# Reordering SyncE's loads of A and x in a fused LoRA and residual kernel

## The reference

```
x = x + einsum('bct,bcd->bdt', x, cond_W[cond_id])
x = x + (x @ W.T + b + 2 * (x @ A[slot]) @ B[slot])      # per sample, slot = adapter id
```

## Time and profile before

| what | value |
|---|---|
| median of 3 runs | 84.96 us (84.85 to 85.13) |
| the profiled execution | 84.99 us |
| its span, first to last instruction | 83.2 us |
| PE busy | 79.4 us (95% of the span) |
| DVE busy | 60.2 us (72%) |
| ACT busy | 52.3 us (63%) |
| POOL busy | 33.7 us (41%) |
| granted TensorE clock | 1.000 |

### The profile page before, as it was taken

One profiled execution on the slowest core, in us unless ns is written; L12 is line 12 of the kernel. 1 busy time (PEld: TensorE's weight loads), 2 busy tenths in 40 slices (PEclk: granted clock), 3 DMA queues, 4 the chain that ended last, 5 costly groups with the idle time before them and its releaser, 6 DMA issues.

```text
span 83.2 us, 2011 instructions
## 1 busy us (share of the span) xinstructions
PE 79.4 (95%) x524; PEld 72.2 (87%) x524; DVE 60.2 (72%) x158; ACT 52.3 (63%) x179; POOL 33.7 (41%) x75
## 2 busy tenths in 40 slices
PE   4999999999999999999999999999999999999970
PEld 2378897899899999999999999999999999999850
DVE  2059765977789687777878787978777777869560
ACT  1553947954867675957666766667585867665620
POOL 6118842871171717080625344351708071304300
PEclk9999999999999999999999999999999999999999
DMA  1899786796987888765768766576764526030334
GB/s 15 287 357 311 203 233 200 211 278 195 335 254 182 262 199 227 194 212 201 176 195 213 219 195 234 156 264 183 230 188 150 174 85 189 17 119 0 126 126 126
DMA packets 16141, 16.07 MB, mean 193 GB/s; under 512 B 10241, under 2 KB 10626, under 8 KB 16130
## 3 DMA queue, kind: packets, MB, share of 16 engines
q1 hardware_dynamic: 14016, 11.67, 47.3%
q0 software_dynamic: 1248, 4.06, 15.7%
q10 hardware_dynamic: 866, 0.21, 1.1%
HBM read 11.74 MB, written 4.19 MB: 191 GB/s over the span
## 4 chain that ended last, share of the span: by engine, by line
PE 82%; SPq 6%; DMA 4%; DVE 2%; issue 2%; ACT 0%; DVEq 0%
PE z_ps L570 49%; PE z_ps L607 9%; PE z_ps L650 5%; PE ht_ps L561 5%; DMA a_raw<-in_lora_a 4%; PE y_ps L622 4%; PE y_ps L618 4%; PE y_ps L620 4%; SPq L237 3%; PE ht_ps L594 2%; PE ht_ps L659 1%; DVE y_sb L555 1%; SPq L227 1%; SPq L234 1%; SPq L257 1%
## 5 line engine op out<-in xcount | busy, mean ns | idle before, releaser
L570 PE MATMUL z_ps<-wa,x_hi 128*128 128x288 f32 (+2 forms) x240 | 50.2, 301 | 0.0
L570 PEld LDWEIGHTS z_ps<-wa,x_hi 128*128 128x128 f32 x240 | 37.9, 188 | 2.0 <-issue 0.5
L570 PE MATMUL z_ps<-wa,x_lo 128*128 128x288 f32 (+2 forms) x120 | 35.2, 295 | 0.0
L570 PEld LDWEIGHTS z_ps<-wa,x_lo 128*128 128x128 f32 x120 | 22.5, 188 | 0.0
L309 POOL CAST m_hi<-m_raw 128x128 fp32r<-128x128 f32 x16 | 4.9, 303 | 35.4 <-ACT m_raw L346 35.4
L300 POOL DMA_INDIRECT b_raw<-in_lora_b,b_index_slot x16 | 16.8, 1048 | 4.4 <-POOL b_index_slot L298 4.4
L490 DVE TENSOR_TENSOR z_lo<-z_ps,z_hi 128x256 fp32r<-128x256 f32 x31 | 11.8, 420 | 6.3 <-ACT z_hi L390 6.3
L390 ACT CAST z_hi<-z_ps 128x256 fp32r<-128x256 f32 x31 | 10.2, 376 | 9.5 <-PE z_ps L607 9.5
L346 ACT COPY m_raw<-w_raw 32x32 f32 x64 | 13.8, 216 | 2.1 <-DVE w_raw L522 1.1
L449 DVE TENSOR_TENSOR x_lo<-x_raw,x_hi 128x512 fp32r<-128x512 f32 x14 | 9.7, 691 | 3.5 <-ACT x_hi L358 3.5
L470 DVE TENSOR_TENSOR b_lo<-b_raw,b_hi 128x512 fp32r<-128x512 f32 x15 | 10.4, 692 | 0.6
(11 more groups left out here) (57 smaller groups left out, 78.3 us busy)
## 6 DMA issues: line engine op xcount, KB each, us to landing
out<-y_sb SPq DMA_DIRECT2D x15, 256.0 KB, 2.5
x_raw<-in_xt SPq DMA_DIRECT2D x14, 256.0 KB, 3.0
a_raw<-in_lora_a SPq DMA_DIRECT2D x60, 32.0 KB, 2.6
first_sb<-in_first SPq DMA_DIRECT2D x2, 384.0 KB, 3.7
first_sb<-in_first SPq DMA_DIRECT2D x3, 256.0 KB, 5.2
b_raw<-in_lora_b,b_index_slot POOLq DMA_INDIRECT x16, 3.7
bias_sb<-in_bias SPq DMA_DIRECT2D x1, 256.0 KB, 3.0
a_raw<-in_lora_a ACTq DMA_DIRECT2D x4, 32.0 KB
```

Of the source, the lines that this page charges most:

```text
L570: done = nc.tensor.matmul(target, (x_hi, x_lo)[part[0]][u % 2][:, k, :], moving(part[1]), start=k == 0 and part == HH, stop=k == KC - 1 an ...
```

## The change

Step u of SP's loop asked for A of tile u + 2 and for x of tile u + 4. It now asks for A of tile u + 3 and for x of tile u + 3, in that order. A of tile 3 and the bias move ahead of the loop, where they are issued in the same place of the order as before. From there the order was: A3, bias, x4, x5, A4, x6, store 0, A5, x7, store 1, A6, x8, store 2. It is now: A3, bias, A4, x4, A5, x5, store 0, A6, x6, store 1, A7, x7, store 2. The number of DMAs, their sizes, their buffers and the conditions inside load_a and load_x are the same.

```diff
             load_a(2)
             load_x(3)
+            load_a(3)
+            sp.dma_start(bias_sb[:, :], bias).then_inc(bias_loaded, 16)
             for u in range(1, TILES):
-                if u + 2 < TILES:
-                    load_a(u + 2)
-                if u == 1:
-                    sp.dma_start(bias_sb[:, :], bias).then_inc(bias_loaded, 16)
-                    load_x(4)
-                if u + 4 < TILES:
-                    load_x(u + 4)
+
+                if u + NA < TILES:
+                    load_a(u + NA)
+                if u + 3 < TILES:
+                    load_x(u + 3)
                 if u >= 2:
                     store_y(u - 2)
             store_y(LAST - 1)
```

## The result

| | before | changed |
|---|---|---|
| median | 84.79 us (84.21 to 85.19, 20 runs) | 85.16 us (84.72 to 86.25, 20 runs) |
| ratio to before, 95% interval | | 1.0055 [1.0031, 1.0079] |
| the profiled execution | 84.99 us, span 83.2 us | 85.14 us, span 83.4 us |

The change makes the kernel 0.55% slower, 0.47 us of 84.79 us. The forecast was 0.11 us faster. Every ratio here is taken over the executions within 1.5% of the fastest of their kernel, which leaves out one of the changed kernel's twenty, the one of 86.25 us. (With more runs the median of before came out 0.17 us lower than the 84.96 us that the forecast stood on; the ratio is what counts here.)

The account below looks back on a forecast made before the run. PE was taken to bound the kernel, except where a load is late before 22 us. Earlier A4 gains 0.23 us, x4 gives back 0.12 us, leaving 0.11 us: 84.85 us against the median of 84.96 us, range 84.68 to 85.65 us.

Parts of the forecast that it names:

- PE bounds, and only the stretch before 22 us can change.: PE is busy 56.98 of 57.00 us from 22 to 79 us, so no load behind 22 us can gain anything.
- The gain is at most 0.23 us.: Iteration 3, transpose_h to lora: PE takes 1.15 us against 0.92 us unhindered; earlier A4 can give back only that 0.23 us.
- A4 comes about 0.95 us earlier and is no longer waited for.: A of tile 4 begins at 14.88 us, lands at 19.97 us, before ACT finishes rounding x at 20.30 us.
- x4 is issued 3.07 us behind the bias and has 2.81 us.: x of tile 4 is issued at 16.87 us instead of 14.40 us; ACT wants it at 19.68 us.
- I take 3.0 us, the bias' row: x4's landing time, taken from the 256 KB bias load behind A3; gives back 0.12 us; break-even 3.11 us, bounds 2.7 to 4.4 us.
- nearest backlog: Reason for x4's 3.0 us: the bias row's bytes, neighbour ahead on the queue and backlog were nearest to x4's new ones.
- lora(2) starts 2.04 us behind the landing, and nothing takes it up.: Iteration 3: PE's lora(2) follows x4's landing by 2.04 us; each further 0.1 us of lateness costs 0.1 us overall.
- x5 costs nothing.: x of tile 5 is issued at 19.81 us and wanted at 24.50 us, 4.69 us later, beyond the longest landing of 4.4 us.
- The later steps are covered.: From iteration 5 on each x has two periods of 4.49 us to land, so its later issue costs nothing.
- x4 is the new stall: Rival: x4 beside the gather of B3 takes 3.8 us, a loss of 0.69 us, total 85.65 us; chance 0.25.
- The full gain: Rival: x4 lands within 2.88 us, the whole 0.23 us stall goes, total 84.73 us; chance 0.25.
- the change that does nothing: Rival: traffic, not issue, sets A4's landing, again near 20.9 us; total stays 84.96 us; chance 0.05.

Follow-up runs that it names:

- old_step1: The changed kernel with step 1 alone in its old order (x4, x5, A4), later steps in the new one; ratio to before 1.0027 [0.9996, 1.0059].
- the five profiles: One profile each of five kernels with the changed order (the first, changed_again, changed_third, dose_x_late, one with extra register loads); mean 0.65 us lost in iterations 3 and 4.
- changed_third: The changed kernel run again without an edit; single time 85.48 us beside 84.58 us of before.
- changed_again: The changed kernel run again without an edit; ratio to before 1.0037 [1.0001, 1.0073], profiled in its slowest execution, 85.69 us.
- dose_x_late: The changed kernel with four 512-byte copies between A and x in steps 6, 8 and 10, delaying x9, x11 and x13; ratio to before 1.0040 [0.9997, 1.0083].
- late_b3: The changed kernel with POOL's gather of B3 moved from 15 us to about 18 us; ratio to before 0.9973 [0.9937, 1.0008], profiled execution 85.80 us.
- late_b3_again: The kernel of late_b3 run once more without a further edit; single time 84.87 us beside 84.58 us of before.

## Why the prediction was wrong, point by point

- *PE bounds, and only the stretch before 22 us can change.* Right: PE is full behind the one late load in every kernel where no later one was late (56.76 of 57.00 us in the changed kernel, where the missing 0.24 us are the end of the wait at 22.24).
- *The gain is at most 0.23 us.* Right for that one execution. As the expected gain it was too much: in old_step1, with A4 in its old place, A4 was not late at all.
- *A4 comes about 0.95 us earlier and is no longer waited for.* Right. Its first copy followed the bias by 0.99 us (14.53 - 13.54; forecast 14.88 - 13.80 = 1.08 us), its last landed at about 19.7, and none of the five profiles shows a wait for A in iteration 3.
- *x4 is issued 3.07 us behind the bias and has 2.81 us.* Nearly right: 2.94 us behind it (16.48 - 13.54). In the five profiles x4 was issued 4.09 to 4.20 us ahead of transpose_h of iteration 3, where the forecast had 4.00 us, so it could take about 3.0 us, not 2.88 us, before PE lost anything (3.73 - 0.70 = 3.03 us in the changed kernel). By this estimate the change would have won the whole 0.23 us if x4 had taken the 3.0 us of the forecast.
- **The step that failed: "I take 3.0 us, the bias' row".** x4 took 3.7 us, and 3.8 us in changed_third, as the x issued at 17.81 had the earlier trace rows. The term was mis-sized by 0.7 us, and that turned 0.11 us of gain into the loss. The break-even of 3.11 us lay so close to the value taken that the sign hung on 0.11 us, while the rows reached to 4.4 us, and rows nearest in place (3.8 us, with the same gather beside) and nearest in backlog (3.0 us) disagreed. The trace of before held one more row, which the prediction left out: the x issued at 21.64, right behind the four copies of A5, took 3.9 us:

```profile
x_raw<-in_xt SPq DMA_DIRECT2D x1, 256.0 KB, 3.9
```

The rule "nearest backlog" had no evidence of its own, and the experiments show that removing parts of the backlog does not reliably shorten the landing.
- *lora(2) starts 2.04 us behind the landing, and nothing takes it up.* Right: 22.24 - 20.21 = 2.03 us.
- *x5 costs nothing.* Wrong in part. It was issued 0.2 to 0.6 us later than forecast (20.04 to 20.45 in the five profiles, against 19.81), and it took 5.0 us in changed_again, beyond the 4.4 us that I took as the longest, and cost 0.61 us there. That is one of five profiles, and of the slowest of twelve executions; in the changed kernel x5 landed in 3.6 us. SP's own issues slipped too: four copies of A, 1.92 us in my sum, took 2.25 us in the changed kernel, and 3.0 us in dose_x_late later on.
- *The later steps are covered.* Right, by dose_x_late.
- *The rivals.* What came is "x4 is the new stall", given 0.25, with its place and its landing time (3.8 us). Its loss was forecast as 0.69 us and is 0.47 us [0.26 to 0.67 us from the interval of the ratio]; in the two profiles it is 0.46 us, since lora came 1.61 us behind transpose_h, against 1.15 us. Of the 0.23 us between 0.69 and 0.46 us, 0.07 us are the shorter landing (3.73 us) and 0.15 us the longer time that x4 had (3.03 us against 2.88 us). That the rival's 3.8 us came so nearly true is luck in part, since its reason, the gather, isn't shown to be the cause. The full gain, given 0.25, and the change that does nothing did not come.

For the rule of the Trainium skill that stood beside that rival ("DMA: Bandwidth & Descriptors", section "Rules for kernel authors": DMAs of SP and GpSimd share 16 engines and interleave): the copies of A4 lean its way, with 2.3 to 4.1 us beside the gather and 1.8 to 2.3 us without, but the ranges meet. For x4 the runs do not decide it. The fit of the same page for GpSimd's path, which carried over to SP's queue gave 2.6 us for 256 KB as an estimate, was too short here: the fastest x4 took 2.7 us, the changed kernel's 3.7 us.

## What to carry to other kernels

When a load is moved back to bring another forward, compare the lead that is left with the longest landing of that size in the trace, and not with the median: a lead of 3.0 us against landings of 2.7 to 4.4 us cost PE 0.1 to 0.7 us in iteration 3 of each of the five profiles of this order. With x5, PE lost 0.65 us on average, nearly three times the 0.23 us that the other load could give back. Even the longest landing of one trace is no bound: 4.4 us before, 5.1 us in late_b3. A median over all x (3.0 us) is made by the quiet steps; of the three x of before issued between 14 and 22 us whose landing is known, two took 3.8 and 3.9 us. The load that is wanted first by its consumer goes first, and this holds within a step as well: here x is rounded before A, and x ahead of A turned a loss of 0.5% into a gain of 0.3%. And a wait seen in one profile is a sample; the load that cost PE 0.2 us before was in time in old_step1, which has the same order up to there.

## What I had not expected of the hardware

- One DMA of 256 KB, issued at 16.2 to 16.9 us, landed in 2.7 us in one execution and in 3.7 us in another of the same kernel on another chip (late_b3, late_b3_again).
- The issue of four 32 KB copies by SP mostly takes 1.9 us, but 2.3 to 3.6 us now and then. These lines of changed_again show both. What holds SP back isn't shown: the DMA engines' share was lower in the slow stretch (0.65 from 21.6 to 25.1 us) than in the quick one (0.77 from 17.8 to 19.9 us). In the two profiles in which x5 took 5.0 and 5.1 us (changed_again, late_b3) the slow issue, 3.5 and 3.6 us, began at 21.60, while x5 was under way:

```profile
17.85 1.99 SPq L237 DMA_DIRECT2D a_raw<-in_lora_a  x4
...
21.60 3.48 SPq L237 DMA_DIRECT2D a_raw<-in_lora_a  x4
```

- PE reaches transpose_h of iteration 2 anywhere between 15.8 and 16.7 us, and that of iteration 3 between 20.3 and 21.2 us, in executions in which it had lost nothing before. That scatter of the start-up is larger than the effect that was to be measured.
